# Recommendation tower on one core: step order turned, a six-slot flat and gated gathers

## The reference

```python
x = layer_norm(dense_t @ Wd.T, gd, bd)                          # 256 -> 128
y = layer_norm(jnp.einsum('bnd,ed->bne', sparse_t, Ws), gs, bs) # 26 rows, 64 -> 128
y = layer_norm(jnp.einsum('bne,pn->bep', y, Wsi), gsi, bsi)     # 26 -> 32 rows
T = jnp.concatenate([x[:, None, :], jnp.swapaxes(y, 1, 2)], axis=1)
Z = jnp.einsum('bnd,bmd->bnm', T, T)                            # 33 x 33 products a sample
out = layer_norm(Z[:, TRIL_I, TRIL_J] @ Wl.T, gl, bl)           # 528 -> 512, 384 kept
h = jnp.maximum(jnp.concatenate([out, r_dense_t], 1) @ W_top1 + b_top1, 0)
h = jnp.maximum(h @ W_top2 + b_top2, 0)
y = h @ W_top3
```

## Time and profile before

| | us |
|---|---|
| median of 3 runs (lowest, highest) | 613.29 (612.51, 615.15) |
| the profiled execution's own time | 615.38 |
| its span, first to last instruction | 613.6 |
| PE busy | 529.8 (86%) |
| DVE busy | 435.1 (71%) |
| ACT busy | 259.3 (42%) |
| POOL busy with gathers | 395.9 (65%) |
| mean granted clock of PE | 0.966 of full speed |

### The profile page before, as it was taken

How to read it: one execution, slowest core, us unless ns; L and a number is a source line. 1 busy time by engine, 2 the same in 40 slices (tenths; PEclk the granted TensorE clock), 3 DMA queues, 4 the chain that set the end, 5 groups by cost and what they waited for, 6 DMA issues and landing times.

```text
span 613.6 us, 15555 instructions
## 1 busy us (share of the span) xinstructions
PE 529.8 (86%) x6347; PEld 376.2 (61%) x6347; DVE 435.1 (71%) x807; ACT 259.3 (42%) x629; POOL 395.9 (65%) x420
## 2 busy tenths in 40 slices
PE   1466788778789999999999999999999999998877
PEld 1353565465556766666667676767667666755645
DVE  3396689778875797679877886779767976795110
ACT  1113155444343554354544554445544543544212
POOL 5777777777777777777777777777777777200000
PEclk9997789989999999999999999999999999999998
DMA  7911113121212131212222131313121212010100
GB/s 235 366 26 27 27 28 59 36 49 28 58 28 58 29 76 27 57 30 52 50 41 45 30 74 28 59 27 75 30 58 27 58 29 58 13 31 9 24 1 0
DMA packets 28566, 31.65 MB, mean 52 GB/s; under 512 B 9928, under 2 KB 20944, under 8 KB 28112
## 3 DMA queue, kind: packets, MB, share of 16 engines
q0 software_dynamic: 13312, 13.66, 12.4%
q1 hardware_dynamic: 15168, 16.99, 10.5%
q10 hardware_dynamic: 16, 0.01, 0.0%
HBM read 23.28 MB, written 0.01 MB: 38 GB/s over the span
## 4 chain that ended last, share of the span: by engine, by line
PE 54%; POOL 21%; issue 12%; ACT 8%; DVE 4%; DMA 1%; ACTq 0%; SPq 0%
POOL emb L262 21%; PE bank_h L391 11%; PE bank_m L414 10%; PE bank_u L358 8%; PE bank_y L369 5%; PE bank_m L442 5%; PE bank_z L379 4%; PE bank_t L334 3%; ACT zt L627 2%; ACT zbig L578 2%; PE bank_g L344 2%; DVE ssum L831 1%; PE bank_m L449 1%; ACT h L636 1%; ACT embt L551 1%
## 5 line engine op out<-in xcount | busy, mean ns | idle before, releaser
L262 POOL DMA_INDIRECT emb<-in_tables,ids x416 | 395.7, 951 | 130.4 <-issue 122.9
L561 ACT COPY us<-bank_u 128x512 f32<-128x512 f32 x64 | 37.5, 586 | 166.4 <-PE bank_u L358 166.4
L831 DVE TENSOR_REDUCE ssum<-sq 128x32 f32<-128x1024 f32 x64 | 77.8, 1216 | 38.3 <-ACT sq L566 37.2
L391 PE MATMUL bank_h<-wz,zr 128*128 128x512 f32 x224 | 104.0, 594 | 0.6 <-ACT zt L627 0.6
L358 PEld LDWEIGHTS bank_u<-mix_w,emb 128*128 128x128 f32 x512 | 84.8, 204 | 26.9 <-DVE emb L814 15.8
L358 PE MATMUL bank_u<-mix_w,emb 128*128 128x192 f32 (+4 forms) x512 | 89.9, 323 | 11.9 <-DVE emb L814 11.8
L825 DVE TENSOR_TENSOR tt<-bank_y,biasc 128x512 f32<-128x512 f32 x128 | 81.4, 678 | 0.0
L369 PE MATMUL bank_y<-us,proj 64*128 64x512 f32 x256 | 75.8, 666 | 5.4 <-DVE tt L825 5.2
L840 DVE TENSOR_TENSOR tt<-tt,bank_g 128x1024 f32<-128x1024 f32 x64 | 78.1, 1220 | 2.2
L566 ACT ACTIVATE sq<-tt 128x1024 f32<-128x1024 f32 x64 | 68.8, 1075 | 12.6 <-DVE tt L825 12.3
L334 PEld LDWEIGHTS bank_t<-eye,emb 128*128 128x128 f32 x208 | 22.9, 147 | 76.5 <-issue 43.1
(11 more groups left out here) (107 smaller groups left out, 523.4 us busy)
## 6 DMA issues: line engine op xcount, KB each, us to landing
emb<-in_tables,ids POOLq DMA_INDIRECT x416
zs<-zbig SPq DMA_DIRECT2D x64, 70.0 KB
zs<-zbig SPq DMA_DIRECT2D x64, 42.0 KB
dense<-in_dense SPq DMA_DIRECT2D x8, 256.0 KB, 4.5
wfull<-in_wfull SPq DMA_DIRECT2D x1, 2048.0 KB, 10.0
wz<-in_wrows SPq DMA_DIRECT2D x1, 1792.0 KB, 13.6
w<-in_w SPq DMA_DIRECT2D x1, 1280.0 KB
w<-in_w SPq DMA_DIRECT2D x1, 512.0 KB
```

Source lines behind the costliest of these rows:

```text
L262: pool.indirect_dma_start(emb[:, e, t, D * a:D * a + D], None, x_in["tables"], bass.IndirectOffsetOnAxis(ap=ids[:, col:col + 1], axis=0),) ...
L391: mm = pe.matmul(bank_h[:, :], zr[:, s, :], wz[:, s, :], start=(s == 0), stop=(s == SLOTS - 1))
L831: dve.tensor_reduce(ssum[:, h % 2, :], sq[:, :, :], AX.X, ALU.add).then_inc(ssum_ok, 1)
```

## The change

It has six parts.
- **Lags and order.** Each stage of a chunk runs fewer steps behind: transposes and gram with the scaling of the rows in step c+1, mix, projection and the chain behind it in c+2, products and their eviction in c+3. PE's order in a step is transposes, mix, gram, projection, products, then flat and top pieces; ACT's and DVE's orders follow. The loop has 76 steps. x is made earlier (`x_of`), and for super 6 and 7 the top stages have steps of their own, counted from `TAIL = 63`.
- **Flat.** Six slots in pieces of 2, 2, 2; the vectors lie in three ranges (`SPAN`), so a unit is moved by twelve DMAs. The last unit's are split between SP and ACT's queue (`move_rest`).
- **Products.** Written for a width `WIDE`, which is 1: the matmuls have the shape that they had. The scratch of `scale_t` is in the products' bank, so it waits for their eviction. `squares` is two instructions, one per half.
- **Gathers.** A chunk's gathers are in two parts (`HALVES`). The first (four gathers) waits for the transposes of two chunks earlier, the second (four or two) for the products of four chunks earlier.
- **Preparation.** `late` on DVE comes at the start of steps 3 to 8, on PE in steps 4 to 7; all four corrections go through one bank.
- **Last super.** Its two halves of 128 samples go through the dense layers one after the other (`last1`, `last2`, `last3`); the first half starts before the last unit's flat.

```diff
-SLOTS = 7
-ROW_LO = 3
-ROW_HI = 5
-SPLIT = LOW * ROW_LO
+SLOTS = 6
+SPAN = ((0, 11, 2, 2), (11, 23, 4, 2), (23, 32, 6, 0))
+BASE = (0, 22, 70)
...
-PIECES = ((0, 3), (3, 5), (5, 7))
+PIECES = ((0, 2), (2, 4), (4, 6))
+HALVES = ((0, 2), (2, 4)), ((4, 6), (6, 7)), ((7, 9), (9, 10)), ((10, 12), (12, 13))
+WIDE = 1
...
-TURN_AT, GRAM_AT, SCALE_AT, MIX_AT, PROJ_AT, CHAIN_AT, PROD_AT, ZOUT_AT = 2, 3, 4, 4, 5, 6, 7, 8
-XCOL_AT, MOVE_AT, FLAT_AT, TURNZ_AT, GAINZ_AT = 6, 11, 13, 16, 17
-DENSEX_AT, TURNX_AT, SUMX_AT = 1, 2, 3
-TOP1_AT, TOP2_AT, TOP3_AT = (22, 23, 24), 28, 29
+TURN_AT, GRAM_AT, SCALE_AT, MIX_AT, PROJ_AT, CHAIN_AT, PROD_AT, ZOUT_AT = 1, 1, 1, 2, 2, 2, 3, 3
+XCOL_AT, SUMCOL_AT, MOVE_AT, FLAT_AT, TURNZ_AT, GAINZ_AT = 2, 3, 6, 8, 11, 12
+TOP1_AT, TOP2_AT, TOP3_AT = (17, 18, 19), 23, 24
 LAST = NSUP - 1
-OPEN_AT, CLOSE_AT = 8 * LAST + 17, 8 * LAST + 21
-STEPS = CLOSE_AT + 4
+TAIL = 8 * LAST + 7
+LAST1_AT, LAST2_AT, LAST3_AT = (TAIL + 5, TAIL + 9), (TAIL + 8, TAIL + 10), (TAIL + 9, TAIL + 11)
+RELU1_AT, RELU2_AT = (TAIL + 6, TAIL + 10), (TAIL + 9, TAIL + 11)
+STEPS = TAIL + 13
...
+def top1_of(s, part):
+    if s == TAIL + (2, 2, 3)[part]:
+        return LAST - 1
...
+                for c in range(4):
                     after(pool, mixed, 4 * (u - EB) + min(c + 2, 4))
-                    after(pool, grammed, 4 * u + c - 3)
-                    for t in range(t0, t1):
-                        for a in range(2):
-                            col = 2 * TILES * u + 2 * t + a
-                            pool.indirect_dma_start(
-                                emb[:, e, t, D * a:D * a + D], None, x_in["tables"],
-                                bass.IndirectOffsetOnAxis(ap=ids[:, col:col + 1], axis=0),
-                            ).then_inc(emb_in[e][c], 16)
...
+                for j in range(4 if u < NU - 1 else 2):
+                    for part in range(3):
+                        sp.dma_start(rows_to(j, part), rows_from(u % 2, j, part)).then_inc(zs_in[u % 2], 16)
...
-                after(pe, t_ok, 4 * u + k + GRAM_AT - CHAIN_AT + 1)
-                after(pe, scaled, 4 * u + k + GRAM_AT - SCALE_AT + 1)
+                after(pe, scaled, 4 * u + k)
...
+            def last1(a):
+                cols = slice(UNIT * a, UNIT * a + UNIT)
+                pe.wait_ge(zt_ok, NU - 1 + a)
+                if a == 0:
+                    pe.wait_ge(scaled, 4 * NU)
...
+                    if a == 0:
+                        o, first = bank_g[:, UNIT * c:UNIT * c + UNIT], (3, 4)
+                    else:
+                        o, first = last_banks[c][:, 0:UNIT], ()
+                    for t in first + (0, 1, 2):
+                        rhs = zt[:, t, cols] if t < 3 else dense[:, LAST % DB, t - 3, cols]
+                        mm = pe.matmul(o, w1[:, t, P * c:P * c + P], rhs, start=(t == 3), stop=(t == 2))
+                    if a == 1:
...
             for s in range(STEPS):
                 c = chunk(s, TURN_AT)
                 if c:
                     turn(*c)
                 c = chunk(s, MIX_AT)
                 if c:
                     mix(*c)
                 c = chunk(s, GRAM_AT)
                 if c:
                     gram(*c)
+                c = chunk(s, PROJ_AT)
+                if c:
+                    project(*c)
+                pd = chunk(s, PROD_AT)
+                if pd:
+                    products(*pd, 0)
+                a = half_of(s, LAST1_AT)
+                if a is not None:
+                    last1(a)
+                if s == TAIL + 5:
+                    open_last()
+                for piece in range(3):
+                    j = top1_of(s, piece)
+                    if j is not None:
+                        top1(j, piece)
+                    u = unit(s, FLAT_AT + piece)
+                    if u is not None:
+                        flat(u, piece)
+                j = top3_of(s)
+                if j is not None:
+                    top3(j)
+                j = top2_of(s)
+                if j is not None:
+                    top2(j)
...
+            def squares(u, h, a):
+                act.wait_ge(y_ok, 2 * (4 * u + h) + a + 1)
...
+            def move_rest():
...
+                for j in range(2, 4):
+                    for part in range(3):
+                        act.dma_start(rows_to(j, part), rows_from((NU - 1) % 2, j, part)
...
+                pj, se, pd = chunk(s, CHAIN_AT), chunk(s, SCALE_AT), chunk(s, ZOUT_AT)
+                if se:
+                    root_e(*se)
+                if pj:
+                    squares(*pj, 0)
+                    squares(*pj, 1)
+                if pd:
+                    products_out(*pd, 0)
+                if pd == (NU - 1, 3):
+                    move_rest()
+                if pj:
+                    root_s(*pj)
...
-                if s == 4:
+                if s == 3:
                     dve.wait_ge(ld_late, 16 * N_LATE)
...
-                if s == 5:
+                if s == 4:
...
+                if s in (5, 6, 7, 8):
+                    q = (3, 1, 1, 0)[s - 5]
+                    dve.wait_ge(late_v, s - 2)
+                    dve.wait_ge(late_p, s - 4)
+                    TT(wz[:, q, :], wz[:, q, :], bank_h[:, :], ALU.add).then_inc(late_v, 1)
...
             for s in range(STEPS):
+                late(s)
                 u = unit(s, TURNZ_AT)
                 if u is not None:
                     stats_h(u)
+                i = x_of(s, 1)
                 if i is not None:
                     stats_x(i)
+                pj, se = chunk(s, CHAIN_AT), chunk(s, SCALE_AT)
+                if se:
+                    times_e(*se)
+                    reduce_e(*se)
                 if u is not None:
                     norm_h(u)
                 if i is not None:
                     norm_x(i)
+                if pj:
+                    add_bias(*pj)
+                if se:
+                    scale_e(*se)
+                if pj:
+                    sum_s(*pj)
+                    scale_t(*pj)
```

More of the change, by code:

```diff
@@ L130, in top3_of, with col_of, gains_z_of, half_of @@
     return j if j is not None and j < LAST - 1 else None
+def col_of(s, lag):
+    if s == lag:
+        return 0
+    u = unit(s, lag - 1)
+    return u if u else None
+def gains_z_of(s):
+    if s == TAIL + 4:
+        return NU - 2
+    u = unit(s, GAINZ_AT)
+    return u if u is not None and u != NU - 2 else None
+def half_of(s, steps):
+    return steps.index(s) if s in steps else None
 def dlrm(nc, x_in, out):
@@ L370, in project, with products @@
                 mm.then_inc(projected, 1)
[L372 to L380, removed]
+            def products(u, h, i):
+                if i == 0:
+                    pe.wait_ge(t_ok, 4 * u + h + 1)
+                    pe.wait_ge(xcol_ok, u + 1)
+                after(pe, zc_ok, NR * (4 * u + h) + i)
+                g0, g1 = ROUNDS[i]
+                for g in range(g0, g1):
+                    for q in range(4 // WIDE):
+                        o = ZC * WIDE * (g - g0)
+                        some = tt[:, u % 2, 4 // WIDE * (8 * h + g) + q, :, :].rearrange("p c w -> p (c w)")
+                        mm = pe.matmul(bank_z[TILE * q:TILE * q + TILE, o:o + ZC * WIDE],
+                                       some[:, C0 * WIDE:ZC * WIDE], some, start=True, stop=True)
                 mm.then_inc(z_done, 1)
@@ L420, in open_last @@
                 pe.wait_ge(y_ok, 8 * NU)
-                pe.wait_ge(u_ok, 4 * NU)
-                pe.wait_ge(embt_ok, 4 * NU)
                 for c in range(4):
                     for t in (3, 4):
[L425 to L429, removed]
-                for c in range(4):
[L431 to L434, removed]
+                        pe.matmul(last_banks[c][:, 0:UNIT], w1[:, t, P * c:P * c + P],
+                                  dense[:, LAST % DB, t - 3, UNIT:2 * UNIT], start=(t == 3), stop=False)
@@ new lines, in last2 @@
+            def last2(a):
+                cols = slice(UNIT * a, UNIT * a + UNIT)
+                pe.wait_ge(h1_ok, 2 * LAST + 1 + a)
+                if a == 0:
+                    pe.wait_ge(y_out, LAST)
+                else:
+                    pe.wait_ge(h2_ok, LAST + 1)
+                for c in range(2):
+                    for t in range(4):
+                        mm = pe.matmul(bank_m[:, UNIT * c:UNIT * c + UNIT], w2[:, t, P * c:P * c + P],
+                                       h1[:, t, cols], start=(t == 0), stop=(t == 3))
+                mm.then_inc(top2_done, 1)
@@ L436, in top2, with last3 @@
+            def last3(a):
+                cols = slice(UNIT * a, UNIT * a + UNIT)
+                pe.wait_ge(h2_ok, LAST + 1 + a)
+                pe.wait_ge(t_ok, 4 * NU)
+                pe.wait_ge(zc_ok, 4 * NR * NU)
+                for c in range(2):
+                    mm = pe.matmul(bank_z[0:1, cols], w3c[:, c:c + 1], h2[:, c, cols],
+                                   start=(c == 0), stop=(c == 1))
```

(10 more changed lines are left out.)

300 lines of the change are left out of this document (166 added, 134 removed).

## The result

The changed kernel takes 607.74 us in the median (603.07 to 610.75, 10 runs), the kernel before 614.89 (10 runs): ratio 0.9888, interval 0.9865 to 0.9911. It is faster by 1.1%, where 593 us and 3.3% were forecast; 607.74 lies just past the upper end of the range. The profiled execution took 608.08 us, its span is 606.3.

The account below looks back on a forecast made before the run. POOL's gather stream was taken to bound the middle: 0 gained there, 6 us of PE's lag traded for 6 of gates, 20.2 from the tail, so the span goes from 613.6 to 593.4 and the time to 593 us; range 584 to 607.

Parts of the forecast that it names:

- the one on the moves: Twelve moves a unit for eight: ACT may wait about 2 us at their copy; taken as 0, bounds 0 to 16.
- POOL's floor: The dense stream of 416 gathers on POOL, 26 per four steps: at least 8.14 us a step.
- the prediction's account of the start: DVE's preparation ahead of its steps 3 and 4 delays products; POOL stalls 4 and 2 us, 6 us never given back.
- SP's part in it: SP issues a move in 0.60 us, so a unit's twelve moves take 7.5 us instead of 5.
- Flat slots: Dropping the seventh flat slot saves 13.8 us of PE time, which buys only the 6 us of PE's lag.
- Gates: Gathers wait for earlier transposes and products: 6 us of stalls at the start (bounds 0 to 12), none in the middle.
- Tail: From the last transposes to the end: 58.9 us for 79.1, a gain of 20.2 us.
- Last transposes: Last transpose at 534.5 us: last gather 526.5, 6 of gates, 2 of landing, no PE lag.
- stated signs of being wrong: POOL waiting in each middle unit, clock well under 0.94 there, last gather past 540, or tail over 65 us.
- Clock: PE idles about 3 us in four steps, the clock drops, PE's work about 1.7 us longer; the gates' slack holds that.
- rival C: Clock and gates feed each other: PE idles, clock falls, products come late, POOL stalls; 633 us, chance 0.08.
- Rival B: PE stays the bound or the gates bite now and then: 10 to 16 us, 603 to 609; chance 0.17.

Follow-up runs that it names:

- e1: The changed kernel with ACT's copy of a unit's moved rows one step later, behind the copy of the mix; 588.41 us, ratio 0.9567.
- e10: The changed kernel with ACT's copy of the moved rows between the copy of the transposes and that of the mix; 592.27 us, ratio 0.9634.
- e2: The changed kernel with the gates on the gathers as in the kernel before, nothing else changed; 606.18 us, ratio 0.9855.
- e9: The kernel before with twelve moves a unit for eight, those of 16 vectors' upper range split in 11 and 5; 616.46 us, ratio 1.0029.
- e4: The kernel before with six of the seven flat slots multiplied, in pieces of 2, 2, 2; 613.02 us, ratio 0.9971.
- e8: The changed kernel with ACT's copy of moved rows a step later, plus a seventh matmul back in each unit's flat; 591.90 us, ratio 0.9597.
- e3: The changed kernel with both ACT's copy of moved rows a step later and the gates of the kernel before; 585.70 us, ratio 0.9529.
- e6: The kernel before with twelve moves a unit for eight, on a chip where PE was slow; 1014.65 us, ratio 1.0101.

## Why the prediction was wrong

**The step that failed** is the one on the moves: "ACT may wait about 2 us at that copy, beside POOL's floor. Nothing in the middle; bounds 0 to 1 us a unit, 0 to 16, I take 0". The wait came as foreseen, 2.4 us. It was not free. What is queued behind it on ACT is the copy of the next chunk's transposes, and in the new order PE's gram wants that within the same step, behind 1.3 us of mix. e1 and e10 show it: 19.3 and 15.5 us less for the same copy at two other places. The prediction had the numbers to see that the room is gone: it gave PE 4.4 us in eight steps, and two waits of 2 to 2.4 us fall into those steps, 4 to 4.8 us. It set the wait against POOL's floor and not against that room, and the upper bound (1 us a unit) had no row behind it.

That comparison tells the direction, not the size: it is at most 0.4 us over the room, some 3 us in the run. The table shows where the rest came from. PE leaves the preparation late in every version with the new order (unit 1 at 56 to 58 us, 50.3 before). In e1 it catches up by unit 3, in 60.9 us where the stream takes 65.0, and then waits for gathers. The changed kernel takes 69.0 us for these two units, with waits of 5.18 and 3.53 us in the gram (a third, of 4.07, follows in unit 3), and never catches up. By unit 3 it is 9.5 us behind e1, by unit 7 15.1; the eight units from there to unit 15 add only 3.1. In these later units the gram waits in every second unit alone, 3.0 to 3.6 us; in the others PE, which has top1's work there, comes to the gram after the copy. In e2, whose gates hardly hold POOL, a unit takes 33.1 us from unit 3 to 15, where the stream needs 32.5: 1.1 us over the room in eight steps. So the prediction's account of the start lacked PE's need to catch up.

- *SP's part in it was undersized.* A move took 0.80 us, not 0.60; twelve 10.0 us, not 7.5. With 2.5 us less a wait of 2.4 us would be hardly left; that is an estimate from these two numbers, no run had faster moves. The row of before was for moves of 16 vectors; the new ones have 11, 12 and 9 (e9).
- *Flat slots: right.* Worth the lag at most. 13.8 us of PE work move the time by 1.7 to 3.5 us (e4, e8), the first with a tail in which the clock fell.
- *Gates: place right, size too large.* POOL waited 3.2 us for products at 56 us (4 at 53 to 57 were forecast), then 0.9 at 79 and 2.4 at 91. In e1, without the wait on ACT, the first of these is 1.4 us, and the gates cost 2.7 us against e3, where 6 were forecast. "No stall there" in the middle holds in e1 (in its whole run 6.7 us of POOL's waits for PE in 15 places, 0.3 of each being plain issue), and not in the changed kernel, in which PE is late.
- *Tail: right, by two errors that offset each other.* 57.7 us from the last transposes to the end, 58.9 forecast. One more wait for ACT, 2.33 us, falls into it; in e1 and e3, without that wait, it is 55.2. The halved layers were faster than forecast (from the last norm's first instruction to the end 12.7 us, not 15.8; last top1 to its relus 3.4 us, not 4.8). The last moves were slower (5.0 us for six, not 3.8).
- *Last transposes:* forecast at 534.5, came at 548.64, in e1 at 531.5. That one difference of 14.1 us is the miss. Less the 1.2 us of the tail it is 12.9 in the span; 1.8 more come from the step to the median, since the profiled execution lay 0.3 us over it and not 2.1. Two of the stated signs of being wrong came: the last gather past 540, and POOL waiting for PE in the middle, in about every second unit.
- *Clock: harmless only while the stream bounds.* After 80 us the granted clock is about half in five stretches of the changed kernel (84 to 91 us, 115 to 125, 152 to 159, 220.6 to 227.3, 357 to 360.3), each beside a wait of PE for ACT of 2.1 to 5.2 us (in the second stretch the clock is down 0.8 us before that wait begins); in e1 it is so in 10 us in all. Where POOL bounds, PE has room for that; here PE bounded, and longer matmuls are lost time: a part of the 6.7 us of busy time under e1. No run separates the clock's share from the wait's. So rival C's loop is there in small, at 220 us: PE idle, clock down, late transposes, POOL stalled 2.57 us and, behind it, twice more 1.0 (0.3 of each is plain issue). It did not feed itself on: the clock is 1.00 again behind it.
- *Rival B* had the right size (10 to 16 us) and named ACT's wait for moves as one of its causes, at 0.17. What stood against it, the 4.4 us of room, is what the wait uses up.

The Trainium skill's page "DMA: Bandwidth & Descriptors", section "Why a DMA increments its semaphore by 16 and not by 1", says that a DMA is split over the largest number of engines, up to 16, that divides the slowest dimension of both its patterns, and that the issuing sequencer itself writes the semaphore for the engines left out. By that rule a range of 16 vectors leaves none out, 11 and 5 leave 5 and 11. The longer issues of e9 agree in direction only, since the move of 5 takes less than that of 11; no run here shows the split itself, nor that it is what costs SP the time.

The version to keep is e3, 585.70 us: 4.7% under the kernel before.

## What to carry to other kernels

A wait of a few microseconds is free only if each instruction queued behind it on its engine is wanted later than that; name the next instruction in the queue and who wants it, and set the wait against that engine's room, not against the bound of the whole. When an order is turned, check the copies that nobody wants soon: each belongs behind those that are wanted at once. Look at the start by itself as well: an engine that leaves it late needs room to catch up, and a wait that the middle could nearly carry takes that room away. And when an engine that gates a stream waits, look at who it waits for before loosening the gate: e2 freed the stream by 16 us and gained nothing that can be measured.

## What the runs showed of the hardware

- A plain DMA between two buffers on the chip takes SP 0.60 us to issue with 16 vectors (partitions) in its range (0.61 in e9), 0.84 with 11, 0.78 with 5 (e9); in the changed kernel, with 11, 12 and 9, 0.80 in the median.
- In the changed kernel the granted clock fell to half beside five of PE's waits for ACT of 2.1 to 5.2 us, and stayed at 1.00 beside others of 1.7 to 2.4 us (at 289.77, 422.67, 488.19 and 552.55 us). At half a projection took 2.08 us for 1.13.
- On one chip the kernel before took 1006.74 us for 615. PE stood still inside runs of small matmuls, up to 2.0 us at a time (e6) and several times in a chunk's 64 records, with nothing to wait for that the profile shows. The granted clock was 0.78 in e6's profile and 0.97 in e9's, the same kernel; PE was busy 743.3 us and 532.0, DVE 439.1 and 434.6, ACT 258.9 and 259.5. The pauses and the low clock come together; what causes the pauses isn't known. The turned order suffered less there (0.82 of the time of before).
